# Counting stage of a four-layer graph network: one 16-bit comparison for the low one-hots of two groups

## The reference, cut to what matters

```python
summed = jax.ops.segment_sum(x[src], dst, num_segments=N)      # layer 0
cnt = jax.ops.segment_sum(jnp.ones((src.shape[0],), x.dtype), dst, num_segments=N)
...
out_deg = jax.ops.segment_sum(ones_e, src, num_segments=n)     # layer 1
agg = jax.ops.segment_sum(h[src], dst, num_segments=n)
```

## Time and profile before

| | |
|---|---|
| median of 3 runs | 4864.38 us (4861.0 to 4865.03) |
| the profiled execution | 4859.22 us, span 4857.5 us |
| setup, up to the first one-hot | 66.3 us |
| counting, to the last one-hot (line 479 and 481) | 66.3 to 660.6 us |
| VectorE busy in these 594.3 us | 593.4 us |
| TensorE / ScalarE busy there | 470.9 / 439.2 us |
| granted TensorE clock there | 0.98 |

### The profile page before, as it was taken

How to read it: one execution, slowest core, us unless ns; L and a number is a source line. 1 busy time by engine, 2 the same in 40 slices (tenths; PEclk the granted TensorE clock), 3 DMA queues, 4 the chain that set the end, 5 groups by cost and what they waited for, 6 DMA issues and landing times. The chain is left out here.

```text
span 4857.5 us, 94822 instructions
## 1 busy us (share of the span) xinstructions
PE 4176.5 (86%) x21268; PEld 2878.9 (59%) x21268; DVE 3853.5 (79%) x9054; ACT 2780.1 (57%) x7136; POOL 2289.0 (47%) x2659
## 2 busy tenths in 40 slices
PE   3878877969999999999999999999996777777776
PEld 1322243546666666666666666666665666666665
DVE  8999956469999999999999999999993545545554
ACT  2777740048888888888888888888881000000000
POOL 1000000035555555555555555555540777777774
PEclk9999978879999999999999999999995555555555
DMA  3111116367887877877877877777760333333332
GB/s 85 80 80 80 80 53 246 148 155 170 173 173 170 174 171 169 174 171 170 174 171 171 174 170 172 173 170 173 171 146 21 80 76 76 76 75 78 76 77 48
DMA packets 576486, 639.86 MB, mean 132 GB/s; under 512 B 204473, under 2 KB 416249, under 8 KB 572483
## 3 DMA queue, kind: packets, MB, share of 16 engines
q1 hardware_dynamic: 517362, 554.10, 48.4%
q0 software_dynamic: 52288, 81.11, 8.0%
q10 hardware_dynamic: 6736, 3.53, 0.3%
HBM read 584.50 MB, written 53.94 MB: 131 GB/s over the span
## 5 line engine op out<-in xcount | busy, mean ns | idle before, releaser
L1332 POOL DMA_INDIRECT attn_rows<-x_twice,attn_idx x808 | 886.7, 1097 | 357.2 <-issue 242.8
L1719 POOL DMA_INDIRECT msg_rows<-a_rows,msg_idx x808 | 781.6, 967 | 363.7 <-issue 220.3
L1359 POOL TENSOR_TENSOR acc_den<-acc_den,attn_sums 128x256 f32 x808 | 553.4, 685 | 387.6 <-DVE attn_z_lo L1577 225.7
L1758 PE MATMUL msg_at_dst<-msg_bwin,msg_pick 128*128 128x64 f32 x1616 | 397.6, 428 | 271.2 <-DVE msg_pick L1784 249.7
L1697 ACT ACTIVATE msg_msg<-msg_pre 128x256 f32<-128x256 f32 x202 | 84.1, 417 | 943.6 <-DVE msg_pre L1798 943.6
L1758 PEld LDWEIGHTS msg_at_dst<-msg_bwin,msg_pick 128*128 128x128 f32 x1616 | 359.8, 328 | 351.6 <-DVE msg_pick L1784 325.3
L1572 DVE TENSOR_TENSOR attn_z<-attn_xt,attn_sh 128x512 f32<-128x512 f32 x808 | 540.4, 690 | 30.0 <-ACT attn_xt L1247 13.0
L1577 DVE TENSOR_TENSOR attn_z_lo<-attn_z,attn_z_hi 128x512 fp32r<-128x512 f32 x808 | 560.3, 693 | 0.2
L1270 ACT CAST attn_z_hi<-attn_z 128x512 fp32r<-128x512 f32 x808 | 496.7, 620 | 82.7 <-DVE attn_z L1572 76.1
L481 DVE TENSOR_SCALAR count_key_hot<-key_iota,key_tab 128x400 bf16<-128x400 f16 x1395 | 496.4, 356 | 0.0
L1361 POOL MEMSET acc_den<- 128x6656 f32 x1 | 5.6, 5645 | 963.9 <-POOLq L93 963.9
(11 more groups left out here) (288 smaller groups left out, 10660.1 us busy)
## 6 DMA issues: line engine op xcount, KB each, us to landing
attn_sh<-in_edge_sh SPq DMA_DIRECT2D x404, 640.0 KB, 8.1
attn_qwin<-q_rows SPq DMA_DIRECT2D x808, 64.0 KB
counts<-chunk SPq DMA_DIRECT2D x15, 3100.0 KB, 9.7
chunk_late<-counts SPq DMA_DIRECT2D x15, 3100.0 KB, 10.5
attn_dst<-dst_near SPq DMA_DIRECT2D x202, 128.0 KB, 3.1
attn_feat<-in_edge_feat SPq DMA_DIRECT2D x404, 64.0 KB
attn_mask<-dst_step SPq DMA_DIRECT2D x202, 128.0 KB, 2.9
msg_dst<-dst_near SPq DMA_DIRECT2D x202, 128.0 KB, 2.9
```

The lines of the kernel that those rows point to most:

```text
L1332: pool.indirect_dma_start(rows[p][:, t, :], None, dram["x_twice"], bass.IndirectOffsetOnAxis(ap=idx[p][:, t:t + 1], axis=0)).then_inc(rows ...
L1359: pool.tensor_tensor(window, window, sums[p][:, :, t, :], ALU.add).then_inc(added, 1)
L1719: pool.indirect_dma_start(rows[p][:, t, :], None, dram["a_rows"], bass.IndirectOffsetOnAxis(ap=idx[p][:, t:t + 1], axis=0)).then_inc(rows_ ...
L1758: mm = nc.tensor.matmul(at_dst[p][:, t * D:(t + 1) * D], pick[p][:, t, :], bwin[p][:, t, :], start=True, stop=True)
```

## The change

The three comparisons for `lo_hot` in each group go. In their place stands one `tensor_tensor` comparison in front of every even group, which makes the six low one-hots of that group and the next. For this `lo_tab` is turned into 16-bit floats with the slots innermost, so that the six numbers of two groups lie side by side; `lo_iota` holds each number six times; and `lo_hot` becomes a buffer of 128 by 6, of which there are three (`PAIRS`). TensorE takes its stationary operand out of this buffer at a step of six elements (12 bytes).

```diff
@@ setup, scalar
             for s in range(SLOTS):
-                nc.scalar.copy(sb["lo_tab"][:, s, :], lo_ps[s][:].rearrange("p k g -> p (k g)")).then_inc(copied, 1)
+                nc.scalar.copy(sb["lo_tab"][:, :, s], lo_ps[s][:].rearrange("p k g -> p (k g)")).then_inc(copied, 1)
@@ setup, gpsimd
-            pool.iota(sb["lo_iota"][:], [[1, P]], base=0, channel_multiplier=0,
+            pool.iota(sb["lo_iota"][:], [[1, P], [0, 2 * SLOTS]], base=0, channel_multiplier=0,
@@ count_and_sum
-        lo_hot = [ph.sb(f"lo_hot{r}", [P, SLOTS, P], BF16) for r in range(RING)]
+        PAIRS = 3
+        lo_hot = [ph.sb(f"lo_hot{r}", [P, P, 2 * SLOTS], BF16) for r in range(PAIRS)]
@@ count_and_sum, vector
             def one_hots(g):
                 if g >= RING:
                     dve.wait_ge(counted, g - RING + 1)
+                if g % 2 == 0:
+                    if g >= 2 * PAIRS:
+                        dve.wait_ge(counted, g - 2 * PAIRS + 2)
+                    both = sb["lo_tab"][:, g:g + 2, :].rearrange("p g s -> p (g s)")
+                    nc.vector.tensor_tensor(lo_hot[g // 2 % PAIRS][:], sb["lo_iota"][:],
+                                            both.unsqueeze(1).to_broadcast([P, P, 2 * SLOTS]), ALU.is_equal)
                 for s in range(SLOTS):
-                    nc.vector.tensor_scalar(lo_hot[g % RING][:, s, :], sb["lo_iota"][:], sb["lo_tab"][:, s, g:g + 1],
-                                            None, ALU.is_equal)
                     ts = nc.vector.tensor_scalar(key_hot[g % RING][:, s, :], sb["key_iota"][:],
                                                  sb["key_tab"][:, s, g:g + 1], None, ALU.is_equal)
@@ count_and_sum, tensor
-                    mm = nc.tensor.matmul(bank[g % 4][:, 0:KEYS], lo_hot[g % RING][:, s, :], key_hot[g % RING][:, s, :],
+                    mm = nc.tensor.matmul(bank[g % 4][:, 0:KEYS], lo_hot[g // 2 % PAIRS][:, :, g % 2 * SLOTS + s], key_hot[g % RING][:, s, :],
@@ program
-                counting_table("lo_iota", [P, P], FP16)
+                counting_table("lo_iota", [P, P, 2 * SLOTS], FP16)
-                counting_table("lo_tab", [P, SLOTS, GK * P])
+                counting_table("lo_tab", [P, GK * P, SLOTS], FP16)
```

## The result

The changed kernel takes 4752.74 us (median of 4 runs, 4749.76 to 4757.03), the kernel before 4862.69 us (4 runs): ratio 0.9769, 95% interval 0.9757 to 0.9782, 110 us less. The forecast was 4756 us. The profiled execution took 4755.38 us, 103.8 us less than that of the kernel before (4859.22).

The account below looks back on a forecast made before the run. VectorE was taken to bound the counting stage; 233 pairs of groups at 0.48 us save 112 us, less 4 us lost at chunk starts: 108 us, so 4864 - 108 = 4756 us. Range 4741 to 4795 us.

Parts of the forecast that it names:

- VectorE bounds the stage: Counting stage, 594.3 us: VectorE is full, so each microsecond taken from it shortens the span until another engine binds.
- The price of the merged comparison: VectorE's 768-element comparison for two groups: 0.46 us, or 0.555 with hops; 0.51 taken.
- one element per cycle: Rival for the merged comparison: it keeps the float32 rate and takes 0.86 us, total 4838 us; chance 0.08.
- The hop of 0.74 ns: Merged comparison's second operand: each read that jumps costs 0.74 ns; one read in three paying adds 0.095 us.
- the sum: VectorE's saving per pair of groups: 0.99 us removed less 0.51 added is 0.48; 233 pairs give 112 us.
- What is given back: First adds of chunks on VectorE wait for TensorE: stalls grow from 1.8 to 5.6 us, 4 us lost.
- The others keep up: Counting stage: TensorE at 0.94 and ScalarE at 1.01 to 1.10 us in 25 groups of 31 stay below the bound.
- the some 220 us of the forecast: TensorE's wait for VectorE was to fall from 334.6 to some 220 us.
- The strided weights: TensorE's weight load at a 12-byte step: 194 ns with a hop on all 128 columns, still below the bound.
- the prediction's other reading: TensorE's strided weight load stays near its contiguous 99 ns, by the Trainium skill's fast weight load.
- The rivals with 0.26 and 0.328 us: Strided weight loads that long make TensorE the bound: 4790 us (partly bound, chance 0.10) or 4882 us (slower, 0.04).
- The setup: GpSimd's larger lo_iota adds at most 0.95 us, VectorE's line 322 may shift; an 8.31 us weight wait hides it.

Follow-up runs that it names:

- e5: Changed kernel with VectorE's add for a group two groups later in its order; ratio 0.9784 to the kernel before, counting stage 478.4 us.
- e9: The changed kernel run again as it is, on chip 7; ratio 0.9795 to the kernel before, counting stage 483.6 us.
- e1: Changed kernel with lo_tab in float32 in place of 16-bit; ratio 0.9947 to the kernel before, counting stage 571.1 us.
- e2: Changed kernel with the slots outermost, lo_hot contiguous for TensorE, second operand at innermost step 0; ratio 0.9948 to the kernel before.
- e6: Changed kernel with ScalarE's 375 row sums for the out-degree left out; ratio 0.9800 to the kernel before, counting stage 483.5 us.
- e4: Changed kernel with lo_hot rows padded from 6 to 16 numbers, weights read at a 32-byte step; ratio 0.9778 to the kernel before.

## Why the prediction was right

1. **VectorE bounds the stage, and each microsecond taken from it is one of the span.** Held within the scatter: the stage fell by 110.3 us (594.3 to 484.0), the time by 110 in the medians. The two profiled executions differ by 103.8 us only. Between the end of the attention and the start of the message layer the changed kernel's took 109.5 us, that of the kernel before 104.0, and e5's and e9's 103.0 and 106.5, so this stretch varies without the change.
2. **The price of the merged comparison.** Two elements per cycle held; the chance of 0.08 for one element per cycle was the right rival to fear, since e1 and e2 show that it comes true as soon as one operand is wide or steps by 0. Within the forecast, the term was mis-sized: I took 0.51 us, halfway between 0.46 and 0.555, and it is 0.47. The hop of 0.74 ns that I read off a reduction at a step of 32 bytes does not show for a repeated row of 12 bytes. The section of the Trainium skill on adjacent pairs of words ("Vector Engine (DVE) Microarchitecture Reference", section 5.2), which I had counted for it, would have made it 0.555 us by my reading; its figures are for 4-byte elements, and the measured 0.47 does not agree. The six low one-hots that go were a little cheaper than the 0.99 us of the sum: 0.97, by the median of 0.162 us from start to start. A pair saves 2.57 - 2.07 = 0.50 us by the steady rows, 116 us in all, in place of 112.
3. **What is given back.** Forecast 4 us, measured 6 to 7 (116 - 110 = 6; 6.6 by the starts). The chunk starts behaved as worked out: stalls of 0.52 and 0.18 us in the idle time, and 0.1 us more each from start to start (0.62 and 0.26 forecast). Against an ordinary add, the 13 first adds came 6.1 us later in the changed kernel and 2.7 us later before (5.6 and 1.8 in the sum), so 3.4 us were lost there. The sum put nothing for the load of the window addresses (line 440): the other stalled adds came 3.7 us later in the changed kernel, 0.5 before. A VectorE with fewer and faster instructions between a load and its add covers less of the load, which is the same kind of effect as at the chunk starts, and it was overlooked.
4. **The others keep up.** Held. TensorE's weight loads waited 142.0 us for VectorE still in the part with adds, 168.2 us in the whole stage, which is less than the some 220 us of the forecast (334.6 before). ScalarE's tally could go without any effect (e6).
5. **The strided weights.** The load rose to 125 ns. It did not stay near 99, the prediction's other reading, but it stayed below the 194 that I had worked out from the hop, and hidden. The rivals with 0.26 and 0.328 us fell, and e4 shows that they fall at 32 bytes too. (The slowest 128-column load before the change was 0.333 us on average, in line 781, not 0.328; nothing hangs on it.)
6. **The setup.** The conclusion held (hidden behind the wait for the weights), one number in it did not: "at most 0.95 us" for the iota took its cost as proportional to the elements. It took 2.53 us, 3.3 ns an element where the plain one took 1.5 ns or less. The pattern of 128 rows of six costs more per element than one row of 128. And the small cast of line 322, which I let shift with it, came 1.4 us later (4.22 us in place of 2.85) but was no longer held, and ended at 4.39 us in place of 10.01.

The two small errors, 4 us too little saved and 2 us too little given back, partly cancel; that 4756 was 3 us from the time is in part luck.

## What to carry to other kernels

Price small instructions on VectorE from start to start, as a fixed part and a rate: here the fixed 0.13 us was most of a 128-element one-hot. The two-tensor comparison reached two elements per cycle here only with three 16-bit operands and an innermost step of 1; lay the repeated index innermost, and make its row even (a row of three lost a quarter of the rate). Let TensorE pay for the layout on the side of the weights, where a step of 12 to 32 bytes hid behind the matmul, not on the moving side, where a step of 12 bytes made the matmul three times as long. And when the bounding engine becomes faster, look at the first instruction of each round that waits for another engine, and at loads that its sequencer starts a fixed number of instructions ahead: moving the add two groups back gave 5 us, and 15 with larger lumps.

## What was not expected of the hardware

- Rows of three 16-bit elements took 2.0 cycles a row in a two-tensor comparison, rows of six and twelve 3.0 and 6.0 (0.47 - 0.07 and 0.87 - 0.07 us for 128 rows).
- A matmul of 400 columns whose moving operand steps by 12 bytes took 0.53 us in place of 0.17, at either granted clock.
- A weight load of 128 bf16 columns took 98, 103, 125, 142 and 145 ns at steps of 2, 6, 12, 24 and 32 bytes.
- One-tensor instructions of VectorE in setup were held by a running instruction of GpSimd: 1.73, 4.86 and 7.16 us for work of 0.17 to 0.26. The Trainium skill ("Advanced Engine Details and Errata", VectorE Performance Modes) says that GpSimd and those VectorE instructions that use two ports block each other over a shared port. These rows agree as far as they go: line 331 with its two tensors and line 329, which reads PSUM, took 0.36 us each while the memset ran that held line 333. Which mode an instruction ran in no row tells.
- The load of eight window addresses (line 440) took 0.60 us mostly, but 9 and 11 of the 51 in the stage took 1.2 to 1.8 us.
- The changed kernel took 4753 us in the result and 5049 us on chip 7, with the counting stage equal to a tenth of a microsecond.
